# GNN message loop: eight target columns and eight source rows fetched by one register load, clear banks sixteen at a time

## What is computed

```
s = leaky_relu(xl[src] + xr[dst], 0.2)
e = einsum('ehc,hc->eh', s, att)
ex = exp(e - segment_max(e, dst)[dst])
alpha = ex / segment_sum(ex, dst)[dst]
out = segment_sum(alpha[:, :, None] * xl[src], dst)    # <- the message step
return out.mean(axis=1) + b
```

## Time and profile before

| what | us |
|---|---|
| three runs | 3326.20, 3327.81, 3335.83 |
| median | 3327.81 |
| the profiled execution | 3325.67, its span 3323.9 |
| message loop of the first GATv2 layer | 1410.7 to 1621.6 |
| message loop of the second GATv2 layer | 2520.9 to 2733.1 |
| TensorE busy over the span | 2516.5 (76%) |
| DVE busy over the span | 2255.7 (68%) |
| ACT busy over the span | 976.7 (29%) |

### The profile page before, as it was taken

How to read it: one execution, slowest core, us unless ns; L and a number is a source line. 1 busy time by engine, 2 the same in 40 slices (tenths; PEclk the granted TensorE clock), 3 DMA queues, 4 the chain that set the end, 5 groups by cost and what they waited for, 6 DMA issues and landing times. The chain is left out here.

```text
span 3323.9 us, 51969 instructions
## 1 busy us (share of the span) xinstructions
PE 2516.5 (76%) x12499; PEld 1545.6 (47%) x12613; DVE 2255.7 (68%) x10815; ACT 976.7 (29%) x2329; POOL 818.4 (25%) x856
## 2 busy tenths in 40 slices
PE   3775894778888787388867888888837884879898
PEld 2443782344444444166734444444425664344444
DVE  5666567868888888844686888888895546242223
ACT  2775991500000000133642000000012345333232
POOL 0000000066666565000003666666610000000000
PEclk8998897899999999699978999999968997989999
DMA  0000601388888886075425888888815542500100
GB/s 24 1 1 3 261 1 31 102 264 278 277 280 278 270 278 227 21 177 162 113 80 195 276 274 281 283 278 279 276 49 140 159 127 53 240 1 7 34 1 19
DMA packets 395805, 507.12 MB, mean 153 GB/s; under 512 B 29035, under 2 KB 331494, under 8 KB 394118
## 3 DMA queue, kind: packets, MB, share of 16 engines
q0 software_dynamic: 66560, 274.39, 24.7%
q1 hardware_dynamic: 327714, 227.61, 24.0%
q10 hardware_dynamic: 1252, 1.80, 0.2%
HBM read 409.08 MB, written 94.61 MB: 152 GB/s over the span
## 5 line engine op out<-in xcount | busy, mean ns | idle before, releaser
L939 POOL DMA_INDIRECT rows<-row_table,idx x832 | 794.0, 954 | 794.4 <-DVE rows L1033 316.9
L990 PE MATMUL z_ps<-xr,hot_ta 128*128 x2400 | 667.8, 385 | 248.5 <-DVE rows L1033 201.0
L1001 PE MATMUL z_ps<-rows,ident 128*128 128x256 f32 x1664 | 570.3, 425 | 4.1 <-issue 2.8
L990 PEld LDWEIGHTS z_ps<-xr,hot_ta 128*128 128x128 bf16 x2496 | 242.6, 97 | 540.3 <-issue 428.9
L2136 PE MATMUL dense_ps<-cnt,h 128*128 128x512 f32 (+1 forms) x1050 | 416.3, 555 | 85.3 <-ACT cnt L2094 81.6
L1033 DVE SCALAR_TENSOR_TENSOR rows<-rows,att_all 128x128 f32<-128x128 f32 x1664 | 423.1, 291 | 47.6 <-remote 26.2
L1059 DVE TENSOR_TENSOR rows<-z_ps,rows 128x256 f32<-128x256 f32 x832 | 348.9, 419 | 116.2 <-PE z_ps L1001 97.7
L1033 DVE SCALAR_TENSOR_TENSOR rows<-z_ps,att_all 128x128 f32<-128x128 f32 x1664 | 411.5, 282 | 19.0 <-issue 18.5
L1376 PE MATMUL acc_m<-xr,hot_m 128*128 x1984 | 341.0, 293 | 74.9 <-issue 55.5
L1376 PEld LDWEIGHTS acc_m<-xr,hot_m 128*128 128x128 f32 x1984 | 282.5, 195 | 140.2 <-issue 134.9
L1017 ACT COPY side<-side_ps 128x96 f32<-128x96 f32 x104 | 24.9, 239 | 1034.5 <-remote 724.7
(11 more groups left out here) (399 smaller groups left out, 3145.3 us busy)
## 6 DMA issues: line engine op xcount, KB each, us to landing
xr<-kept_rows SPq DMA_DIRECT2D x124, 512.0 KB
kept_rows<-rows SPq DMA_DIRECT2D x416, 128.0 KB
spread_a<-rel_rows SPq DMA_DIRECT2D x208, 128.0 KB
counts_line<-counts SPq DMA_DIRECT2D x1, 19550.0 KB
counts<-counts_line SPq DMA_DIRECT2D x6, 3200.0 KB
rows<-row_table,idx POOLq DMA_INDIRECT x832
row_table<-xl_ring SPq DMA_DIRECT2D x50, 258.0 KB
rows<-row_table SPq DMA_DIRECT2D x32, 320.0 KB
```

The costliest lines, as they stand in the source:

```text
L939: nc.gpsimd.indirect_dma_start(out=rows[:, u, :], out_offset=None, in_=table, in_offset=bass.IndirectOffsetOnAxis(ap=c.idx[:, n:n + 1], ax ...
L990: nc.tensor.matmul(ps[:, n % Z, :], hot, tile[:, m, 0:HC], start=m == 0, stop=False, skip_group_check=True)
L1001: nc.tensor.matmul(ps[:, n % Z, HALF_C:HC], c.ident[:, :], rows[:, n % ROWS, HALF_C:HC], start=False, stop=True, skip_group_check=True).th ...
```

## The change

`sums_at` and `rows_at` are replaced by `steps_at`, which loads all 16 numbers of a half at once, at slot 4 of the half before. The first eight are used with the bounds that `load` gives them, the target's. For the other eight the bound is narrowed by `nc.s_assert_within`, called without the argument that leaves the check out. `AHEAD` goes from 8 to 16, so `clears_at` loads 16 bank numbers for each 48 slots in place of 8 for each 24.

```diff
-    AHEAD = 8
+    AHEAD = 16
...
-                    def sums_at(n):
-                        return load(0, n * M_PE, M_PART, mybir.EngineType.PE, BANKS * BANK - AGG)
-
-                    def rows_at(n):
-                        return load(0, n * M_PE + M_PART, M_PART, mybir.EngineType.PE, (M_PART - 1) * (C + 1))
+                    def steps_at(n):
+                        steps = load(0, n * M_PE, M_PE, mybir.EngineType.PE, BANKS * BANK - AGG)
+                        return steps[0:M_PART], [nc.s_assert_within(v, 0, (M_PART - 1) * (C + 1))
+                                                 for v in steps[M_PART:M_PE]]
...
-                    sums_next, rows_next, clear_next = sums_at(0), rows_at(0), clears_at(0)
+                    (sums_next, rows_next), clear_next = steps_at(0), clears_at(0)
...
-                        elif n + 1 < HALVES and u == 2:
-                            sums_next = sums_at(n + 1)
                         elif n + 1 < HALVES and u == 4:
-                            rows_next = rows_at(n + 1)
+                            sums_next, rows_next = steps_at(n + 1)
```

## The result

The changed kernel takes 3468.87 us (median of 4 runs, 3467.41 to 3470.38) against 3331.14 us of before, measured beside it. The ratio is 1.0418, with a 95% interval of 1.0405 to 1.043: it is 138 us slower. The forecast was 3458 us.

The account below looks back on a forecast made before the run. TensorE's sequencer was taken to bound both loops. Fewer loads -19, checks +159 and swallowed wait -10 us sum to +130 us on 3327.81, so 3458 us; 80% for +50 to +190 us, 3375 to 3520 us without the outer rivals.

Parts of the forecast that it names:

- The bound: In both L1376 matmul loops, TensorE's sequencer sets the time, half of it register loads: 9.8 of 9.9 us per three halves.
- Fewer loads: On PE's queue 290 loads become 146; 144 gone at 0.13 us each save 19 us, 28 at the far end.
- The checks: Behind each 16-register load on PE's queue, 992 pairs at 0.16 us add 159 us, from 71 to 210.
- The part that is swallowed: Early in each loop, TensorE's wait for the source-row DMA shrinks by 5 us, 10 us for both loops.
- Sum: Whole program: -19 + 159 - 10 = +130 us, put on the 3327.81 us median, gives 3458 us.
- The flat load price: Rival on PE's queue: a load costs the same whatever its size; +49 us in sum, 3377 us; 6%.
- Nearly free checks: Rival behind PE's 16-register loads: pairs under 0.019 us, kernel faster, about 3303 us; 4% faster, 3% tie.
- Dearer checks: Rival on PE's queue: a pair costs 0.3 us; +266 us in sum, 3594 us; 7%.
- the array as the bound: Suspect in both loops: TensorE's array sets the pace; it needs 6.6 of 10.0 us per three halves; no chance given.
- The clock: Rival in both loops: TensorE falls to 1.2 GHz, three halves need 13.3 us of array; adds under 20 us; no chance given.

Follow-up runs that it names:

- the thin clears: The kernel before the change with its 332 clearing matmuls one column wide in place of 387, PE's queue unchanged in number and kind: 3331.29 us, ratio 1.0001.

## Why the prediction was right, step by step

*The bound.* The sequencer of TensorE was named as the bound, at full price for all that is added to its queue. Three runs bear it out from three sides: the array's work cut with no effect (ratio 1.0001), the checks added alone (+163 us), and the straight line through half the checks.

*Fewer loads.* The 16-register load was put at 1.12 us from loads of 4 and 8; its median is 1.122. Loads of 4, 8 and 16 registers, 0.333, 0.597 and 1.122 us, lie on one line of 66 ns a register and 69 ns a load; with 32 registers it would give 2.18, and 2.14 was measured. The term was sized at 19 us with 28 as its far end, and the version without checks gained 26. So it was sized too low by some 7 us, and the reading behind the far end was wrong. The loads of 0.77 us were taken for collisions with other readers of SBUF, of which a merged pair would meet one in place of two. In the traces they are the loads at which the table row changes (before: 0.655 us at most without a change, 0.76 or more with one). Merging the two loads of a half leaves all of those in place; it was `AHEAD` = 16 that took 40 of the 84 away. This also accounts for why a load that was split off cost 0.127 us while one that went away saved 26 / 144 = 0.18: the price of a load can be the same in both, and the rest are the row changes. Why a row change costs 0.18 us was not looked into.

*The checks.* The term was 159 us, at 0.16 us a pair. The trace has 0.172 us at the median and 178 us in all, inside the inner bounds of 0.126 and 0.194 a pair. The reasoning behind the middle was partly off. The ALU_OP on PE takes 34 ns, not longer than SP's 36, and the check takes 18. What PE is slower at is the step from one to the next: 95 and 77 ns, against 63 and 67 in the raw starts of SP's ALU_OP and MOVE. The rule of the Trainium skill ("Vector Engine (DVE) Microarchitecture Reference", "Instruction fetch and dispatch (NX sequencer)"), by which only SP's sequencer has the short dispatch path, would put PE above SP's row, and the trace agrees in the direction: 0.172 against 0.130 us a pair. That it is the dispatch which takes the difference was not shown by any run.

*The part that is swallowed.* 10 us were counted, and the two waits of the earlier trace rows shrank by 4.0 and 4.6 us, 8.6 together. The cause that was given, the large transfers of `own_rows`, is borne out by the experiment that spreads them.

*Sum.* From the traces of both kernels: the loads, each to the start of the next instruction, went from 207.9 to 179.7 us, the pairs add 178, the wait for source rows lost 8.6, and a wait of 3.0 us for the one-hot matrices is gone. That is -28 + 178 - 9 - 3 = +138, against 138.7 us in the loops and +138 in the medians. The forecast of +130 came closer than its terms, and that was luck: the gain from the loads was too small by 9 us and the loss from the checks by 19, so the two errors partly cancelled. The loops took 280 and 282 us where 276 was foretold, and nothing was added outside them that the change could be blamed for.

*The rivals.* The flat load price fell with the 1.122 us of the load and with the 26 us of the version without checks. Nearly free checks fell with the 0.172 us, and the point from which they would have decided was about right: a gain of 26 us over 992 pairs would be used up at 0.026 us a pair. The figure of 48 ns an instruction that spoke against them rests on 25 instructions for the stretch of the earlier trace rows, three for each slot and clear and one wait, which neither the program nor the trace shows in this form. What the trace shows are steps of PE's queue: 142 ns for a slot, 120 for a clear and 106 for the wait, which fill the same 1.2 us. Dearer checks fell as well, and the array as the bound fell with the thin clears.

*The clock.* The granted clock of the loops went from 0.98 and 0.97 to 0.88 and 0.87. TensorE ran at the lower of its two levels, 1.2 GHz, more often than before. It cost next to nothing: in the steady part, halves without a load of clear banks take 4.28 us at the median where the mean granted clock was under 0.75 (24 of them) and 4.26 where it was at full level (63). That fits the rival as it was put. At the lower level three halves need 8 x 1.61 = 12.9 us of the array, and the queue takes 13.5.

## What to carry to other kernels

Where an engine's idle time ends with "issue" while others wait for it, its sequencer is the suspect: add up the register loads and register instructions of its queue by their rows, and see whether the sum fills the stretch. A register load is paid by the register more than by the load, so merging loads saves little (0.13 us for each that goes), and here a load from another row of the table than the last one took 0.18 us extra. A bound that is narrowed on a loaded value may quietly put two instructions on the queue for each value. Compare the instructions of the built programs before the times: the diff reads as if it only took loads away, and the queue has 1984 instructions of comparison and check more and 144 loads fewer.

## What the runs showed of the hardware

On TensorE's sequencer a register comparison of 34 ns and a check of 18 ns hold the queue for 172 ns at the median; durations alone would have given 52. A register load takes 66 ns for each register and 69 ns on top, from 4 to 16 registers (2.14 us with 32), and in these traces 0.18 us more if its row of the table is not that of the load before, which was seen at every such load of the loops but not tested by an edit. And a wait that looked small in the profile of before, 14.3 us for a DMA in both loops, was worth 18 us once the sequencer was relieved. It is set by transfers that were issued earlier, and it grows as TensorE comes to it sooner: 1.6 us at the fifth half of both loops with the checks alone, 14.3 before, 19.3 without checks.
